# Earlier gathers, scatters, norm steps and weight turns at the seams of a twelve-stage routed transformer

## The reference, cut to what matters

```python
x = x + 0.5 * L0_ffn(ln(x));  x = x + L0_attn(ln(x));  x = x + 0.5 * L0_ffn(ln(x))
x = x + 0.5 * L1_ffn(ln(x));  x = x + L1_attn(ln(x));  x = x + 0.5 * L1_ffn(ln(x))
x = x + 0.5 * L2_ffn(ln(x));  x = x + L2_attn(ln(x));  x = x + 0.5 * L2_ffn(ln(x))
x = x + 0.5 * L3_ffn(ln(x));  x = x + L3_attn(ln(x));  x = x + 0.5 * L3_ffn(ln(x))
```

```python
# L1_ffn: two of 8 experts for a token, two layers with a Silu between, H = 512
logits = silu(xt @ rw1 + rb1) @ rw2 + rb2;   idx = top_k(logits, 2)
h  = silu(einsum('nd,edh->enh', xt, we1) + be1);  eo = einsum('enh,ehd->end', h, we2) + be2
y  = xt + einsum('ne,end->nd', softmax(where(chosen, logits, -inf)), eo)
# L2_ffn: gate, up and down are each a linear layer over two of 8 experts, I = 512
inter = silu(moe_linear(xt, router_gate, w_gate)) * moe_linear(xt, router_up, w_up)
d  = moe_linear(inter, router_down, w_down)
# L2_attn ("neighbour attention"): differences of neighbouring tokens in a window of 8,
# guided by 64 trajectories
traj = (blended * combined).sum(axis=2) / weight_sum
# L3_ffn: 2 shared and 16 routed experts, two of the 16 for a token
h  = silu(einsum('td,edm->tem', flat, wg_r)) * einsum('td,edm->tem', flat, wu_r)
out = shared + einsum('tem,emd->td', h * comb[:, :, None], wd_r)
```

## Time and profile before

| | us |
|---|---|
| median of three runs | 2706.76 (2706.0 to 2707.62) |
| the profiled execution, its own time | 2690.79 |
| its span in the trace | 2689.0 |
| TensorE matmul busy | 2395.6 (89%) |
| VectorE busy | 1644.0 (61%) |
| ScalarE busy | 1453.9 (54%) |
| GpSimd busy | 784.1 (29%) |
| mean granted clock of TensorE | 0.948 of full |

### The profile page before, as it was taken

One profiled execution on the slowest core, in us unless ns is written; L12 is line 12 of the kernel. 1 busy time (PEld: TensorE's weight loads), 2 busy tenths in 40 slices (PEclk: granted clock), 3 DMA queues, 4 the chain that ended last, 5 costly groups with the idle time before them and its releaser, 6 DMA issues. The chain is left out here.

```text
span 2689.0 us, 41502 instructions
## 1 busy us (share of the span) xinstructions
PE 2395.6 (89%) x13335; PEld 1229.5 (46%) x13424; DVE 1644.0 (61%) x2954; ACT 1453.9 (54%) x3263; POOL 784.1 (29%) x828
## 2 busy tenths in 40 slices
PE   7978999998797799999999998987998777998888
PEld 3435666765696222222222224873444553443333
DVE  5777988975332888888888852331444531445554
ACT  3672233233464388787878786654444335554444
POOL 1224665650243500000000002244544014443112
PEclk9988999999898699999999999998999878999999
DMA  5353223301474312020111003866766008665112
GB/s 161 87 152 110 90 86 105 101 24 43 133 214 130 98 22 34 3 42 15 23 22 15 2 4 112 265 203 233 239 217 224 1 27 281 233 215 162 30 35 65
DMA packets 205398, 286.49 MB, mean 107 GB/s; under 512 B 24688, under 2 KB 128624, under 8 KB 202448
## 3 DMA queue, kind: packets, MB, share of 16 engines
q1 hardware_dynamic: 186792, 233.94, 28.8%
q0 software_dynamic: 18432, 50.36, 6.0%
HBM read 176.17 MB, written 107.73 MB: 106 GB/s over the span
## 5 line engine op out<-in xcount | busy, mean ns | idle before, releaser
L3198 DVE TENSOR_REDUCE big<-psum 128x2 f32<-128x1024 f32 x512 | 603.9, 1221 | 76.5 <-PE psum L2995 72.8
L3152 ACT ACTIVATE probs<-psum 128x512 f32<-128x512 f32 x1024 | 553.3, 600 | 140.1 <-PE psum L3016 127.3
L3016 PE MATMUL psum<-big,k_ops 128*128 128x512 bf16 x944 | 294.7, 387 | 12.1 <-ACT probs L3152 7.3
L1735 PE MATMUL psum<-big,turned 128*128 x480 | 233.7, 616 | 16.6 <-ACT turned L1895 13.6
L1834 PE MATMUL psum<-big,probs 128*128 128x512 f32 x512 | 232.7, 606 | 6.6 <-DVE down_sum L2015 6.6
L3016 PEld LDWEIGHTS psum<-big,k_ops 128*128 128x128 bf16 x1024 | 81.4, 97 | 333.4 <-ACT probs L3152 260.5
L1429 ACT ACTIVATE hidden<-psum,big 128x128 f32<-128x128 f32 x480 | 136.1, 370 | 100.1 <-PE psum L1322 100.0
L1903 ACT ACTIVATE big<-psum 128x512 f32<-128x512 f32 x240 | 139.6, 597 | 90.4 <-PE psum L1735 62.1
L644 POOL DMA_INDIRECT linear_rows<-desk_tokens,linear_row x128 | 126.1, 985 | 212.8 <-DVE linear_row L620 109.9
L2995 PE MATMUL psum<-big,w_A_or_L_A 32*128 32x512 bf16 x1024 | 164.7, 398 | 26.0 <-DVE big L3198 14.4
L1685 POOL DMA_INDIRECT big<-linear_y,linear_row x128 | 126.7, 990 | 193.8 <-PE psum L1735 122.8
(11 more groups left out here) (500 smaller groups left out, 4028.7 us busy)
## 6 DMA issues: line engine op xcount, KB each, us to landing
linear_y<-big SPq DMA_DIRECT2D x240, 256.0 KB, 4.1
big<-in_experts SPq DMA_DIRECT2D x120, 322.0 KB, 3.8
big<-step_rows SPq DMA_DIRECT2D x16, 1024.0 KB, 4.6
qkv_chunks<-big SPq DMA_DIRECT2D x48, 256.0 KB, 2.3
big<-qkv_chunks SPq DMA_DIRECT2D x16, 768.0 KB
big<-linear_rows SPq DMA_DIRECT2D x48, 256.0 KB, 4.1
big<-since_rows SPq DMA_DIRECT2D x32, 256.0 KB
big<-row_store SPq DMA_DIRECT2D x32, 256.0 KB, 5.3
```

Source lines behind the costliest of these rows:

```text
L1735: pe.matmul(k.bank[bank_of(n, m)][:, :], turned[:, q % 2, t % 4, :], w["up" if r else "gate"][:, bass.ds(experts[r][t] * TB, TB)], start=T ...
L3016: pe.matmul(k.bank[2 + m % 3][:, :], k_ops[:, g % 2, h, kt * P:(kt + 1) * P], q_ops[:, g % 2, i % QB, h, :], start=True, stop=True).then_i ...
L3152: act.activation(probs[:, kt % 2, h, :], k.bank[2 + m % 3][:, :], ACT.Exp, scale=SCALE).then_inc(expd.sem, 1)
L3198: dve.tensor_reduce(into, k.row_pair[hp].rearrange("p (h t) -> p h t", h=2), AX.X, ALU.max).then_inc(row_max.sem, 1)
```

## The change

There are four edits. The first is in stage 5 alone (`linear` is set where L2 follows): in the last block the eight gathers are paced by `reached(3, 2 + step // 2)` where it was `reached(3, 3 + step)`. The second is in stage 8 alone, where the stage before has not done all scatters: what was left over had one gate per step from tile 0 on; now steps 4 to 7 have no gate and steps 8 to 15 wait for tiles 0, 1, 2, 3, 5, 6, 7 and 8. The scatters of block 1 behind them wait for tiles `min(10 + step * 5 // 4, 29)` where it was `8 + step * 4 // 3`. The third moves `pe_turn_back` behind the products up and down in both L3 stages. The fourth is in A2: four scatters where there were eight, and another order of the lists of TensorE, ScalarE and VectorE at its end.

```diff
@@ sorted_silu_ffn, GpSimd
-                    reached(n, 9 + step * 3 // 4 if n + 1 < NB else 3 + step)
+                    reached(n, 9 + step * 3 // 4 if n + 1 < NB else 2 + step // 2 if linear else 3 + step)
                     gather(pool, n - 1, step, step + 1)
@@ sorted_linear_ffn, GpSimd
-            route.pool_scatter(pool, 0, begun.scattered, 4 * TPB, lambda step: at_tile(0, step - begun.scattered))
-            scatter(1, lambda step: at_tile(0, 8 + step * 4 // 3 if late else 4 + step * 8 // 5))
+            route.pool_scatter(pool, 0, begun.scattered, 4 * TPB, lambda step: at_tile(0, (step - 2 * TPB) * 5 // 4) if step >= 2 * TPB else None)
+            scatter(1, lambda step: at_tile(0, min(10 + step * 5 // 4, TILES - 1) if late else 4 + step * 8 // 5))
@@ shared_routed_ffn, TensorE
-                if routed(i, 3):
-                    route.pe_turn_back(pe, routed(i, 3))
                 up(i)
                 if i > 0:
                     down(i - 1)
+                if routed(i, 3):
+                    route.pe_turn_back(pe, routed(i, 3))
@@ window_attention, GpSimd
-            ahead.pool(pool, 2 * TPB)
+            ahead.pool(pool, TPB)
@@ window_attention, ScalarE
             ahead.act(act, "square")
+            ahead.act(act, "deviation")
             mix(3)
             guide_out(2)
-            ahead.act(act, "deviation")
+            ahead.act(act, "logits")
+            ahead.act(act, "tokens")
             guide_out(3)
-            for step in ("logits", "tokens", "exp"):
-                ahead.act(act, step)
+            ahead.act(act, "exp")
@@ window_attention, VectorE
             invert_sums(3)
+            ahead.dve(dve, "invert")
             add_to_x(1)
-            ahead.dve(dve, "invert")
+            ahead.dve(dve, "norm")
             add_to_x(2)
-            ahead.dve(dve, "norm")
+            ahead.dve(dve, "choose")
             add_to_x(3)
-            ahead.dve(dve, "choose")
             ahead.dve(dve, "weigh")
```

More of the change, by code:

```diff
@@ L2512, in _ @@
             window_sums(3)
+            ahead.pe(pe, "variance")
             add_up(1)
             turn(2)
-            ahead.pe(pe, "variance")
+            ahead.pe(pe, "spread")
             add_up(2)
-            ahead.pe(pe, "spread")
-            turn(3)
             ahead.pe(pe, "logits")
             ahead.pe(pe, "tokens")
+            turn(3)
+            ahead.pe(pe, "by_token")
             add_up(3)
-            ahead.pe(pe, "by_token")
             pe.wait_ge(ahead.route.tokens_out.sem, ahead.route.tokens_out.at(0))
```

## The result

| kernel | runs | median, us | ratio of runs to before (95%) |
|---|---|---|---|
| before, beside the changed kernel | 12 | 2707.8 | 1 |
| changed | 12 | 2704.9 | 0.9980 (0.9972 to 0.9989) |

By the ratio the change made the kernel 5.4 us faster (3.0 to 7.6). Forecast were 14.3, and the time of 2704.9 is outside the range that ended at 2700.5. One execution of before took 2873.3 us and, like a few in the later sessions, is left out of the ratios as far slower than the rest. The profiled execution took 2703.5 us with a span of 2701.7 and a mean granted clock of 0.944.

A forecast was written before the change was run, and what follows sets the result against it. Only gaps of TensorE, the busiest engine, could be won: 4.3 (stage 5) + 2.0 (A2, stage 8) + 2.6 and 5.4 (L3) = 14.3 us, off the 2706.76 median: 2692.5 us, range 2687.5 to 2700.5.

The forecast's parts named there:

- stages 5 and 6: Seam of stages 5 and 6: earlier gathers let GpSimd's scatters end 4.3 us earlier, its tail unchanged; 4.3 us gained.
- A2 and stage 8: End of A2 and first block of stage 8: four scatters fewer and reordered lists gain 2.0 us, between 0 and 3.3.
- stage 9: First L3 stage: up and down run in TensorE's gaps before the weights' turn; 1.0, 1.0 and 0.6, together 2.6 us.
- stage 11: Second L3 stage: 3.7 us from products run in the gaps plus 1.7 for a clock fall expected to vanish; 5.4 us.
- the stretches are the same work, so I take the difference off: Whole kernel: the 14.3 us gain read from the 2690.8 us trace is subtracted from the 2706.76 median, giving 2692.5.
- rival (a): Stage 5's seam does not move because its tail waits for something other than the scatters; 10.0 us left, 2696.8; chance 0.13.
- 6.38 us is three times A2's 1.9: Argument that stage 5's seam may not move: GpSimd's idle time there against the shorter tail after A2's scatters.
- The 0.5 taken off for the clock: Stage 8: 0.5 us deducted from 2.5 because a new 5 us wait could prolong the half-clock stretch.
- (b): Stage 11's clock fall stays and stage 8 loses its 2.0 us to a longer half-clock stretch; 2696.2 us; chance 0.18.
- (c): Gains in stage 8 and L3 are eaten by other waits, only stage 5 gives 4.3 us; 2702.5 us; chance 0.10.
- (d): L3 stages: turned rows come 1.6 us late at six places, 9.6 us lost, kernel slower at 2710.1; chance 0.07.

The follow-up runs named there:

- f0: The changed kernel again, unchanged, beside before at 2691.2 us: ratio to before 0.9946, 14.5 us faster.
- h0: The changed kernel, unchanged, in the fourth session, before at 2689.1 us: ratio to before 0.9962, 10.2 us faster.
- e0: The kernel before, unchanged, for a second trace: ratio 1.0005, span 2688.0 us.
- g0: The changed kernel, unchanged, in the third session, before at 2713.0 us: ratio to before 0.9969, 8.4 us faster.
- g3: Before with only the moved turns in the L3 stages and GpSimd's scalings cut to 16 columns: ratio to before 0.9962, 10.3 us faster.
- g1: Before with only the gathers' gates of stage 5 changed, third session: ratio to before 0.9998 (0.9983 to 1.0013).
- group A: Runs and traces from sessions where the kernel before took 2688 to 2691 us; the first trace of before is counted here.
- group B: Runs and traces from sessions where the kernel before took 2707 to 2713 us, the result's own included.
- g2: Before with GpSimd's scalings in the L3 stages cut from 512 to 16 columns, the rest left out: ratio to before 0.9980, 5.4 us faster.
- e1: Before with only the gathers' gates of stage 5 changed, first session: ratio to before 0.9998, 0.5 us faster.
- f1: The changed kernel without the gathers' edit of stage 5: ratio to before 0.9976, 6.5 us faster than before.
- e3: Before with only the turns moved behind up and down in both L3 stages: ratio to before 0.9988, 3.2 us faster.
- h2: Changed kernel with stage 8's first six stores ahead of the up router's slots, scatter gates kept: ratio to before 0.9922, 10.8 us below the changed kernel.

## Why the prediction was wrong

The sum, term by term, from traces of the same group (f0 and h0 against the first trace and e0; the first trace of the changed kernel and g0 against g3 for stages 5 and 6, and g1 for the rest):

| | forecast | group A | group B |
|---|---|---|---|
| stages 5 and 6 | −4.3 | −4.6 | −2.4 |
| A2 and stage 8 | −2.0 | −2.6 | +1.1 |
| stage 9 | −2.6 | −2.5 | −1.8 |
| stage 10 | 0 | +0.9 | +1.7 |
| stage 11 | −5.4 | −4.3 | −4.8 |
| sum | −14.3 | −13.1 | −6.2 |
| timed | | −14.5, −10.2 | −5.4, −8.4 |

The column of group B rests on few traces: of the kernels without the edit in question, stages 5 and 6 took 484.5 us in g3 and 486.3 in g2, and A2 with stage 8 395.5 in g1, 392.8 in g2 and 396.4 in g3. Either entry may be off by 2.

**The base.** The step that failed first is "the stretches are the same work, so I take the difference off": 14.3 us of gains read from one trace were taken off the median of executions that took 16 us longer, as if each term were worth the same there. The median itself held (2706.76, then 2707.8; the range's lower end adds up to 2687.8 and not 2687.5, on which nothing hangs). The sum did not: on group B the traces give 6.2 us and the timed runs 5.4 and 8.4, on group A 13.1, 14.5 and 10.2. Of the 8.1 us missing on B, 3.1 are in A2 and stage 8, 1.9 in stages 5 and 6, 1.7 in stage 10, 0.8 in stage 9 and 0.6 in stage 11.

What sets the groups apart is not the kernel. The unchanged stage 3 took 173.5 to 177.8 us in the thirteen traces of group A and 178.5 to 181.4 in the five of B, the unchanged stage 4 780 to 784 and 785 to 786. From f0 to the first trace of the changed kernel, the same kernel in both, 25.3 us are added: 10.2 in stage 5, 5.8 in stage 3, 3.1 in stage 6, 2.9 in stage 8, 1.9 in stage 4 and 1.3 in stage 10. Stages 0 to 2, 7, 9 and 11 are equal to 0.8 us. So most of it lies in the stages that sort through HBM. Why is open.

**Stage 5.** Forecast: "Their count stays, so GpSimd's end is 4.3 earlier", and the tail stays. On group A both hold in the traces (4.35 at the seam in e1). On group B GpSimd's end is no longer what sets the seam. In stage 5 its five traces show waits without a recorded releaser, 19 to 30 us on VectorE and 6 to 28 on ScalarE, and these are longer waits and not only unnamed ones: VectorE is idle for 123 to 131 us of stage 5, and for 102 to 112 in the thirteen traces of group A, where no such wait stands in it. In four of the five, TensorE's gap before stage 6 is down to 3.1 to 4.0 us, in g3 without the edit too, and in both traces of the full change GpSimd itself is held 2.3 or 2.5 us among its scatters. This is rival (a), in a form that I had not given: not that the tail waits for a landing, but that the other engines are no longer 10 us ahead. The rival's "6.38 us is three times A2's 1.9" also set two different spans side by side: from GpSimd's last end to the place where all engines meet it is 5.5 us in stage 5.

What the edit is worth is less clear. In the traces of group A stages 5 and 6 together took 465.1 to 468.6 us with it (six traces) and 469.6 to 475.1 without (seven); on group B 481.8 to 485.5 with it and 484.5 and 486.3 without. Timed, the edit alone gave 0.5 and 0.5 us, the step in company 8.1 and −0.8, with a mean of 2.1 and some 3 to 5 us of uncertainty each. So the traces of group A show a gain of the size forecast, and the timed runs neither confirm nor exclude it.

**A2 and stage 8.** Where the clock falls at the same point of A2 (the first trace and f1), the chain moved as worked out: the first scatter comes 3.63 us earlier after A2's start (3.6 forecast), TensorE's first slots 3.48 (3.3). By other pairs of traces it is 3.1 to 5.0 us. 2.0 was right to 0.6 on group A. The 0.5 taken off for the clock had the wrong sign: the new wait "can only prolong" the stretch at half clock (0.50), I wrote, but it lasted 27.3 us in all eight traces with the old lists of A2 and 23.9 in all ten with the new. On group B stage 8 lost another 3 us between 50 and 70 us after its start, in both traces of the changed kernel against f0 and not in g1. Part of it is a later stretch at half clock, 6.83 us long (first line, the changed kernel) where it is 3.41 in f0 (second line), worth up to 1.7; TensorE also stands still twice for about 0.5 us just before it, in both. What makes these is open.

```profile
2274.23:2281.06 6.83, 6.08 (x18) 2.73 (x19) 0.34 (x2) 2.67 (x6) 0.97 (x1) 0.50 0.77 242
```

```profile
2253.12:2256.53 3.41, 3.41 (x15) 1.68 (x15) 0.00 (x0) 1.47 (x3) 0.97 (x1) 0.50 0.65 209
```

I also left the larger stall where it was, the one behind SyncE's list: 9.93 us of TensorE's time at L162 in the trace of before. I had read ScalarE's wait of 11.50 and not asked who waits for ScalarE.

**L3.** 2.6 came as 2.5 on group A and 1.8 on B. In e3 the third place of stage 9 lost its 0.6 to the hold by a scaling. Of 5.4 in stage 11, 4.3 or 4.8 came. Against g1, the first two places of the changed kernel gave 0.9 each where 1.0 was forecast, and the third gave 2.9 where 3.4 was, the clock included: in all four traces of the full change TensorE still waits 1.46 to 1.74 us there, where 0.4 was forecast, with L307 at 0.96 to 1.24 us and L313 at 0.79 under two scalings. In e3 it was the second place that still waited, 1.37, with L317 at 1.20 under a scaling. The sum had VectorE's chain at the time that it had in one trace, and took no account of what GpSimd does beside it.

The clock's fall behind the third turn is gone in all four traces of the full change, as forecast. But I had priced stage 10 at nothing. It took 26.0 to 26.3 us in eight of the eleven traces with the moved turns and in one of the seven without them (g2), and 24.5 to 24.8 in the others. In the nine long ones, and in no other, a stretch of 3.4 us at half clock begins 7.4 to 7.9 us after the stage does. Half of 3.4 us is 1.7, as long as the stage got. Which execution has it is not foretold by any row: f0, f1 and g3 have neither this fall nor the one of stage 11.

For the scaling the Trainium skill has the rule, in "SBUF — State Buffer", section "SBUF: two separate sides": the shared port pair is an exclusive lock, which a VectorE instruction with two SBUF inputs takes against a GpSimd one that reads SBUF. The traces agree: the held instructions end 0.02 to 0.09 us after the scaling, and take 0.16 to 0.27 again with the short one. The forecast used this section only for the descriptors of the scatters, where the cost was as small as the rows had it (in f0 the longest of the sixteen took 1.118 us again).

**The rivals.** (b), the clock going against it, is half true: the fall in stage 11 went, another came in most traces, and on group B a stretch in stage 8 got longer. (c) has the time, 2702.5 against 2704.9, by other reasons, which is luck. (d) did not happen: no turn was so late that TensorE waited for the turned rows or for GpSimd.

## What to carry to other kernels

Where a trace and the timed runs differ by more than the runs scatter, find out which stages differ before subtracting one from the other; a gain at a seam is priced for the conditions of that trace only. When an engine waits long for a buffer, follow who stands behind it: here six stores moved ahead of four fetches in SyncE's list (h2) were worth 10.8 us beside the 10.2 of the four edits together. Before moving an instruction to hide a chain on VectorE, look at what runs on GpSimd beside the chain.

## What the runs showed of the hardware

- A VectorE instruction of 0.16 to 0.23 us with two inputs in SBUF, started while a GpSimd tensor_tensor of 1.27 us runs, ends 0.02 to 0.09 us after it, so it takes up to 1.3 us. In the sixteen traces with the whole scaling this holds for 110 of 113 instructions on eight lines (L261 to L317) of stages 9 and 11. Two of the others started in the scaling's last 0.1 us and kept their 0.22, and one started with the scaling (h2) and kept its 0.21, while the scaling took 1.34. Instructions with one input (L259, L306, L309, L315) kept 0.18 to 0.22.
- The same kernel took 2688 to 2691 us in three sessions and 2707 to 2713 in two (the one of the result counted). Most of the difference sits in the stages that scatter and gather through HBM; the traces of those two also lack a quarter of the events of finished DMAs (15,252 to 15,606 against 20,210 to 20,240). Whether missing events and longer stages have one cause is open, and so is whether it is the chip or the session.
- The same kernel in two sessions with like times of before was 28.0 and 19.4 us faster than it, with intervals of about 4 us on either side: sessions differ by more than one session's interval says.
